# Cross-attention row maxima from the high parts alone, two heads at a time, in a fused decoder layer

## The reference, cut to what matters

```python
k = src_key.reshape(b, s, NUM_HEAD, HEAD_DIM)          # 8, 512, 8, 64
q = tgt_trans.reshape(b, t, NUM_HEAD, HEAD_DIM)
scores = jnp.einsum('bthd,bshd->bhts', q, k) / np.sqrt(HEAD_DIM)
scores = jnp.where(src_mask[:, None, None, :] == 0, -jnp.inf, scores)
attn = jax.nn.softmax(scores, axis=-1)
tgt_update = jnp.einsum('bhts,bshd->bthd', attn, v).reshape(b, t, OUT_SIZE)
```

## Time and profile before

| | |
|---|---|
| median of 3 runs | 2109.98 us (2108.62 to 2110.39) |
| the profiled execution: its own time | 2113.0 us |
| its span, first to last instruction | 2111.2 us |
| mean granted clock of TensorE over the span | 0.975 of full speed |
| PE busy | 1977.4 us (94%) |
| DVE busy | 1397.5 us (66%) |
| ACT busy | 784.5 us (37%) |
| rounds of `phase_b` | first from about 985 us; the loop's seven take 132.8 us each |

### The profile page before, as it was taken

How to read it: one execution, slowest core, us unless ns; L and a number is a source line. 1 busy time by engine, 2 the same in 40 slices (tenths; PEclk the granted TensorE clock), 3 DMA queues, 4 the chain that set the end, 5 groups by cost and what they waited for, 6 DMA issues and landing times. The chain is left out here.

```text
span 2111.2 us, 35399 instructions
## 1 busy us (share of the span) xinstructions
PE 1977.4 (94%) x13100; PEld 1057.0 (50%) x13100; DVE 1397.5 (66%) x1826; ACT 784.5 (37%) x1209; POOL 216.2 (10%) x416
## 2 busy tenths in 40 slices
PE   6999999999999999876789999999999999999998
PEld 5555455545555445533454545545455454554543
DVE  4279978987797879996666555565555555646531
ACT  3322222122222222112655536355363562645622
POOL 0000122003200321031000010100100001000010
PEclk8999999999999999986999999999999999999999
DMA  6112222122122212315641131410414104141010
GB/s 210 36 46 70 76 66 65 61 71 75 55 64 66 81 56 66 111 59 120 194 86 51 27 94 27 96 50 19 96 34 96 50 12 100 36 96 30 1 40 20
DMA packets 151569, 143.10 MB, mean 68 GB/s; under 512 B 55529, under 2 KB 108777, under 8 KB 151426
## 3 DMA queue, kind: packets, MB, share of 16 engines
q1 hardware_dynamic: 147056, 140.58, 23.5%
q10 hardware_dynamic: 4370, 0.34, 0.2%
HBM read 94.75 MB, written 33.55 MB: 61 GB/s over the span
## 5 line engine op out<-in xcount | busy, mean ns | idle before, releaser
L1459 DVE TENSOR_TENSOR p_lo<-k,p_hi 128x1024 f16<-128x1024 f32 x128 | 156.8, 1225 | 194.0 <-ACT p_hi L1347 194.0
L1148 PE MATMUL b_ff<-x2T_hi,w1T_hi 128*128 128x512 f16 x512 | 194.9, 381 | 1.9 <-DVE x2T_lo L1459 1.9
L1504 DVE CUSTOM_DVE_ANT_0 junk<-b_sx,mneg 128x512 f16<-128x512 f32 x256 | 175.7, 686 | 30.4 <-issue 22.3
L1148 PE MATMUL b_ff<-x2T_lo,w1T_hi 128*128 128x512 f16 x512 | 194.9, 381 | 0.0
L1148 PE MATMUL b_ff<-x2T_hi,w1T_lo 128*128 128x512 f16 x512 | 194.7, 380 | 0.0
L1379 ACT ACTIVATE k<-b_st,mbias 128x512 f32<-128x512 f32 x256 | 161.5, 684 | 14.1 <-PE b_st L1192 14.0
L572 PE MATMUL pj_b<-winT_hi,xT_hi 128*128 128x512 f16 x384 | 146.5, 381 | 7.6 <-DVE xT_lo L790 7.6
L1347 ACT ACTIVATE p_hi<-k 128x1024 f16<-128x1024 f32 x128 | 135.3, 1057 | 44.1 <-PE b_av L1207 41.7
L814 DVE TENSOR_TENSOR prod<-q,k 128x4096 f32<-128x4096 f32 x32 | 141.2, 4411 | 8.8 <-ACT bd L696 8.8
L572 PE MATMUL pj_b<-winT_lo,xT_hi 128*128 128x512 f16 x384 | 145.9, 380 | 0.0
L572 PE MATMUL pj_b<-winT_hi,xT_lo 128*128 128x512 f16 x384 | 145.9, 380 | 0.0
(11 more groups left out here) (262 smaller groups left out, 4285.2 us busy)
## 6 DMA issues: line engine op xcount, KB each, us to landing
cn<-in_ctx_dram SPq DMA_DIRECT2D x64, 256.0 KB, 2.8
k<-kT_scratch SPq DMA_DIRECT2D x24, 512.0 KB, 7.8
xn<-in_x_dram SPq DMA_DIRECT2D x32, 256.0 KB, 2.9
xres<-in_x_dram SPq DMA_DIRECT2D x32, 256.0 KB, 2.9
x_scratch<-x SPq DMA_DIRECT2D x32, 256.0 KB, 2.0
q<-x_scratch SPq DMA_DIRECT2D x8, 1024.0 KB, 5.6
q<-x_scratch SPq DMA_DIRECT2D x32, 256.0 KB, 4.2
out_dram<-q SPq DMA_DIRECT2D x32, 256.0 KB, 4.4
```

Of the source, the lines that this page charges most:

```text
L1148: mm = pe.matmul(out, a, c, start=(start and n == 0), stop=end)
L1459: dve.tensor_tensor(dst, bank, hi, ALU.subtract).then_inc(out, 1)
L1504: dve.tensor_tensor_reduce(junk[:, :], sx_b[tt % 2][:, :], mneg[:, :], 1.0, NEG, ALU.add, ALU.max, mx[:, h % 2, tt:tt + 1]).then_inc(s["sx ...
```

## The change

The scores that serve only to find the row maxima are made from the high parts alone: queries high times keys high, with a contraction of 64. Their operands are the natural layouts, `qn` and a new tile `kn` (keys of one batch, high part, 512 KB, loaded by a transfer of its own ahead of the three others). Two heads lie in the two halves of the 128 partitions, so one call of `scores(b, p, tt)` issues two matmuls, one on rows 0 to 63 and one on rows 64 to 127 of the array, for the heads 2p and 2p+1, into two banks at once. The scores that the probabilities are made of are not changed.

`maximum_rows` now serves a pair of heads: `mz` has two columns for the two heads, four matmuls give two rows, and one ACT copy writes both rows for both heads (2 partitions x 1024 elements, in place of 1 x 512). `k2` gets a one in row 64 for even heads and in row 65 for odd ones.

A pair's scores must be complete before its first head goes on. So four calls (eight matmuls, eight DVE passes) now stand ahead of head 0, where one head's four stood: calls 0 and 1 within the last query product, call 2 behind it, and call 3 inside `heads`, after the first feed-forward tile. Calls 1 and 3 go to the banks `b_st`. During the heads, two calls stand in each of the heads 0 to 5 and none in 6 and 7.

```diff
+    kn = sb("kn", [P, 4, B], F16)
...
-    mz = sb("mz", [P, 8, DV], F16)
+    mz = sb("mz", [P, 8, D2 + 2], F16)
...
+    score_banks = lambda p, tt: st_b if p == 0 and tt % 2 else sx_b
...
+                sp.dma_start(kn[:, :, :], kn_in[b, 0]).then_inc(s["k_ld"], 16)
                 sp.dma_start(k1[0:D2, :, :], k_in[b, 0]).then_inc(s["k_ld"], 16)
...
-            def scores(b, h, half):
-
-                for tt in (2 * half, 2 * half + 1):
-                    if h or tt >= 2:
-                        pe.wait_ge(s["sx_max"], 32 * b + 4 * h + tt - 1)
-                    pe.matmul(sx_b[tt % 2][:, :], q1[:, h, tt * P:(tt + 1) * P], k1[:, h, :], start=True,
-                              stop=True).then_inc(s["sx_filled"], 1)
-
-            def maximum_row(b, h):
-                pe.wait_ge(s["negm"], 8 * b + h + 1)
+            def scores(b, p, tt):
+
+                if p:
+                    pe.wait_ge(s["sx_max"], 32 * b + 8 * p + 2 * tt)
+                elif tt >= 2:
+                    pe.wait_ge(s["sx_max"], 32 * b + 2 * tt - 2)
+                for a, bank in enumerate(score_banks(p, tt)):
+                    head = slice(a * D2, (a + 1) * D2)
+                    mm = pe.matmul(bank[:, :], qn[0][head, p, tt * P:(tt + 1) * P], kn[head, p, :], start=True,
+                                   stop=True)
+                mm.then_inc(s["sx_filled"], 1)
+
+            def maximum_rows(b, p):
+                pe.wait_ge(s["negm"], 4 * b + p + 1)
                 for tt in range(4):
-                    mm = pe.matmul(mr_b[0:DV, tt * P:(tt + 1) * P], mz[:, 4 * (h % 2) + tt, :], ident16[:, :],
+                    mm = pe.matmul(mr_b[0:D2 + 2, tt * P:(tt + 1) * P], mz[:, 4 * (p % 2) + tt, :], ident16[:, :],
...
                 feed_forward1(ff, 0)
                 pe.wait_ge(s["q_masked"], 4 * b + 4)
-                maximum_row(b, 0)
+                scores(b, 0, 3)
+                maximum_rows(b, 0)
                 for h in range(H2):
                     for g, (i, _) in enumerate(GROUPS):
                         for a in range(2):
-                            if h + 1 == 2 * i + a:
+                            if h == 2 * i + a:
                                 pe.wait_ge(qs_ld[g][a], 48 * (b + 1))
-                    if h + 1 < H2:
-                        scores(b, h + 1, 0)
+                    following = h // 2 + 1
+                    if following < 4:
+                        scores(b, following, 2 * (h % 2))
                     transposed_scores(b, h, 0)
...
+                    if h % 2 and following < 4:
+                        maximum_rows(b, following)
                     if h + 1 < H2:
-                        maximum_row(b, h + 1)
                         feed_forward1(ff, 2 * h + 2)
...
-                pe.wait_ge(qs_ld[0][0], 48 * (b + 1))
+                pe.wait_ge(s["q_hi"], 4 * b + 2)
                 scores(b, 0, 0)
+                scores(b, 0, 1)
                 queries(b, 3, slice(8, None))
-                scores(b, 0, 1)
+                scores(b, 0, 2)
...
-            def maximum_row(b, h):
-                act.wait_ge(s["mr_filled"], 8 * b + h + 1)
-                act.activation(q2[D2:DV, h, :], mr_b[D2:DV, :], ACT.Copy).then_inc(s["mr_copied"], 1)
+            def maximum_rows(b, p):
+                act.wait_ge(s["mr_filled"], 4 * b + p + 1)
+                act.activation(q2[D2:D2 + 2, 2 * p:2 * p + 2, :],
+                               mr_b[D2:D2 + 2, :].unsqueeze(1).to_broadcast([2, 2, B]),
+                               ACT.Copy).then_inc(s["mr_copied"], 1)
...
             def heads(b, ff):
                 w1_low(ff, 0)
+                maxima(b, 0, 3)
...
-                maximum(b, 0, 0)
+                maxima(b, 0, 0)
                 queries_low(b, 2)
+                maxima(b, 0, 1)
                 queries_masked(b, 3)
-                maximum(b, 0, 1)
+                maxima(b, 0, 2)
                 queries_low(b, 3)
```

More of the change, by code:

```diff
@@ L974, in phase_b @@
     junk = sb("junk", [P, B], F16)
-    mx = sb("mxb", [P, 2, 4], F32)
+    mx = sb("mxb", [P, 4, 2], F32)
     ph = pair("p", [P, 4, B])
@@ L1014, in phase_b @@
     k_in = w.kT_d.rearrange("b z (h d) s -> b z d h s", h=H2)
+    kn_in = w.kT_d.rearrange("b z (o p) s -> b z p o s", p=P)
     v_in = w.v_d.rearrange("b z (st p) o -> b z p st o", p=P)
@@ L1186, in transposed_scores @@
                     if st == 0:
-                        pe.wait_ge(s["mr_copied"], 8 * b + h + 1)
+                        pe.wait_ge(s["mr_copied"], 4 * b + h // 2 + 1)
                     if h or st >= 2:
@@ L1271, in heads @@
                         values(b, h - 1)
-                    if h + 1 < H2:
-                        scores(b, h + 1, 1)
+                    if following < 4:
+                        scores(b, following, 2 * (h % 2) + 1)
                     feed_forward1(ff, 2 * h + 1)
                     transposed_scores(b, h, 1)
+                    if h % 2 and following < 4:
+                        maximum_rows(b, following)
                     if h + 1 < H2:
-                        maximum_row(b, h + 1)
                         feed_forward1(ff, 2 * h + 2)
@@ L1306, in queries_and_first_scores @@
                     pe.wait_ge(s["x2t_lo"], 4 * ff + 2)
[L1307 to L1308 removed]
+                pe.wait_ge(s["k_ld"], 64 * (b + 1))
+                pe.wait_ge(s["q_hi"], 4 * b + 2)
                 scores(b, 0, 0)
+                scores(b, 0, 1)
                 queries(b, 3, slice(8, None))
[L1311 removed]
+                scores(b, 0, 2)
             def x2_transposes(b):
@@ L1326, in _ @@
             queries_and_first_scores(0, None)
-            pe.wait_ge(s["rows_made"], 3)
+            pe.wait_ge(s["rows_made"], 4)
             pe.wait_ge(s["made"], 2)
@@ L1402, in heads @@
                     exponentials(b, h, 1)
-                    if h + 1 < H2:
-                        maximum_row(b, h + 1)
+                    if h % 2 and h + 1 < H2:
+                        maximum_rows(b, h // 2 + 1)
                     exponentials_high(b, h, 1)
@@ L1432, in _ @@
             act.wait_ge(s["cols_ld"], 32)
-            act.wait_ge(s["rows_made"], 3)
+            act.wait_ge(s["rows_made"], 4)
             heads(0, None)
@@ L1495, in queries_low, with maxima @@
                 low(qn[1][:, i, :], qf[i % 2][:, :], qn[0][:, i, :], s["q_hi"], 4 * b + i + 1, s["q_lo"])
[L1497 to L1502, removed]
-                    stand_alone(dve, alone["dve"])
[L1504 to L1508, removed]
+            def maxima(b, p, tt):
+                dve.wait_ge(s["sx_filled"], 16 * b + 4 * p + tt + 1)
+                for a, bank in enumerate(score_banks(p, tt)):
+                    if p or tt or a:
+                        dve.wait_ge(s["sx_max"], 32 * b + 8 * p + 2 * tt + a)
+                    stand_alone(dve, alone["dve"])
+                    dve.tensor_tensor_reduce(junk[:, :], bank[:, :], mneg[:, :], 1.0, NEG, ALU.add, ALU.max,
+                                             mx[:, tt, a:a + 1]).then_inc(s["sx_max"], 1)
+                if tt == 3:
+                    dve.wait_ge(s["sx_max"], 32 * b + 8 * p + 8)
+                    dve.tensor_scalar(mz[:, 4 * (p % 2):4 * (p % 2) + 4, D2:D2 + 2], mx[:, :, :], -1.0, None,
                                       ALU.mult).then_inc(s["negm"], 1)
@@ L1541, in heads @@
                 w1_low(ff, 0)
+                maxima(b, 0, 3)
                 for h in range(H2):
-                    if h + 1 < H2:
-                        maximum(b, h + 1, 0)
+                    following = h // 2 + 1
+                    if following < 4:
+                        maxima(b, following, 2 * (h % 2))
                     if h:
                         normalized(b, h - 1)
-                    if h + 1 < H2:
-                        maximum(b, h + 1, 1)
+                    if following < 4:
+                        maxima(b, following, 2 * (h % 2) + 1)
                     exponentials_low(b, h, 0)
@@ L1599, in _ @@
                     dve.wait_ge(s["rows_made"], 2)
-                    dve.tensor_scalar(k2[D2:P, :, :], q2[D2:P, :, :], w.ident[D2:P, D2:D2 + 1], None,
-                                      ALU.add).then_inc(s["rows_made"], 1)
+                    for a in range(2):
+                        dve.tensor_scalar(k2[D2:P, a::2, :], q2[D2:P, a::2, :], w.ident[D2:P, D2 + a:D2 + a + 1], None,
+                                          ALU.add).then_inc(s["rows_made"], 1)
                 weights_low(lo, om_b[n % 4], high, s["wq_hi"], n + 1, s["wq_lo"])
```

## The result

The changed kernel takes 2149.4 us (median of 4 runs, 2145.7 to 2153.6) against 2110.2 us in 4 runs of the kernel before: a ratio of 1.0189, with a 95% interval of 1.0176 to 1.0202. It is 39 us slower; the forecast was 2141 us, 31 us slower. The profiled execution took 2149.8 us, with a span of 2148.0 and a mean granted clock of 0.969.

What follows compares the result with a forecast made beforehand. PE, busy 94% of the span, plus its waits, bound the kernel; DVE had no slack at the front. Seven rounds at +4.3 us (+30) and batch 0's +1.3 made +31.5: 2141 us, 8-in-10 range 2124 to 2157.

Steps and rivals of the forecast that it cites:

- the rivals: Clock stays up, 2132 us (14%); pairs run one after another, 2154 (14%); front cheap, kernel faster (3%); no change (3%).
- its own terms: Bounds on front (3.0 to 4.2), copy (0.59 to 1.18), clock (0 to 1.7) and batch 0: 2130 to 2150 us.
- The front: Round's start, before head 0's transposed scores: four more DVE passes and a longer copy delay them, +3.66 us a round.
- The heads: Within heads 0 to 6, shorter and longer stretches together: a gain of 0.86 us a round.
- The even stretches: Last transposed scores to values, heads 0, 2, 4: PE's own 4.75 us sets them, -0.39 us each.
- the odd ones: Last transposed scores to values, heads 1, 3, 5: ACT's longer copy makes the chain 5.59 us, +0.45 each.
- Head 6's -0.61: Last transposed scores to values in head 6: the chain sets it and loses its copy, -0.61 us a round.
- The pair absent behind its values: Matmuls behind head 6's values, on PE's path, no longer there: -0.43 us a round.
- The pairs: Two half-depth score matmuls side by side between full ones: no gain, +0.01 us each, +0.1 us a round.
- The clock: Behind the front's wait the clock drops to 1.2 GHz in 8 of 10 rounds: +1.35 us a round.
- The loads ahead of this cost nothing: Key loads ahead of the front: 512 KB more hidden by projections and output_rest; uncovered, up to 7.8 us.
- Batch 0: Same front, but a later wait for a transfer, whose issue moves by 1.3 us, leaves +1.3 us, bounds 0 and +4.

Runs made afterwards that it cites:

- Experiment 2: Changed kernel without DVE's four passes over the second head's scores in each first pair, the negation using the first head's maxima for both: 2117.3 us, 1.0037.
- Experiments 3 and 4: ACT's row copy moved behind p_hi: in the changed kernel (3), 2140.8 us, 1.0148; in the kernel before (4), 2098.7 us, 0.9940.
- Experiment 6: Changed kernel with its order, but each score matmul at full depth of 128 from q1 and k1: 2150.7 us, 1.0190.
- experiment 7: Changed kernel with both matmuls of a call at depth 64 on the same half of the array's rows: 2165.3 us, 1.0257.
- experiment 5: Changed kernel with 13 matmuls of unused result in each batch, between the last pair and the maxima matmuls: 2136.8 us, 1.0121.
- Experiment 1: Kernel before with only the new 512 KB kn transfer for each batch, loaded, waited for and never read: 2117.9 us, 1.0032.
- experiment 8: Changed kernel with kn loaded for batch 0 only, later batches taking maxima from batch 0's keys: 2145.6 us, 1.0169.

## Why the prediction was right, and where it was short

The result lies 8 us above the forecast and inside the range, and none of the rivals came in. It is at the upper end of the 2130 to 2150 that the prediction gave its own terms. With all its bounds at their ends together these come to about 2116 and 2153, so that span was drawn narrower than its sum, without saying how.

- **The front: right.** The wait at `mz` is 3.15 us (3.2 forecast), the copy 1.01 us (1.04), the delay +3.72 (+3.66). Experiment 2 takes the passes away and the delay with them, but for 0.8 us: 0.4 of it is the longer copy, and the rest stays open.
- **The heads: right.** The even stretches end on PE's own 4.75 us, as forecast, the odd ones on the chain through ACT at 5.64 (5.59). Experiments 3 and 4 show that chain by moving the copy off it. Head 6's -0.61 was -0.49. The chain sets it, as forecast, for `values` still waits 0.19 us for p_lo there (the next row), but the chain got shorter by 0.49 only. The pair absent behind its values gave -0.44 (-0.43). What the even heads gain, the odd ones give back, +0.3 us a round more than that.

```profile
1336.38 0.20 PE L1212 MATMUL b_av<-v_hi,p_hi 128*128 128x65 f16 x1 [0.19 <-DVE p_lo L1473]
```

- **The pairs: right.** 0.63 us for two, by the way in and out. Experiment 6 shows that full depth costs the same, and 7 that the gain of working side by side is real and is just eaten up. The rule that a change of tiling mode drains TensorE (the Trainium skill, "TensorEngine Tiling (Array Packing)", Key Properties) has its price here: 0.10 us on each side of a pair.
- **The clock: right mechanism, too small.** I took 1.67 us at 8 rounds in 10, or +1.35. It was every round, and 2.1 us a round by experiment 5; in the round shown the low level held for 6.8 us, as in five of the seven, and for 3.4 in the others. The gap I had read the loss from the earlier trace rows was one of the short kind.
- **The step that failed: "The loads ahead of this cost nothing".** The cover was there, but the transfer lengthens the queue into the start of the next round, and PE's first instruction there comes late. Experiment 1 gives 7 us for it alone, 4.6 of them in the wait at the loop's way back and 2.7 in the second wait, which the changed kernel has not; experiment 8 gives some 4 within the changed kernel, and "last" shows +0.7 a round. I had priced a transfer by who waits for its data, and nobody does; what waited was behind it. The first instruction starts a fixed time behind a packet of instructions, and that packet comes later where the loop has the transfer. That the two go together is shown; what links them is not.
- **Batch 0**: +0.6 measured, +1.3 forecast. The front is 4.8 us longer there, and waits for transfers behind it give most of that back: the longest shrank from 4.0 us to 0.8, since the transfer's issue had moved by 1.6 us only (1.3 in the prediction).

Clock (+5 us in seven rounds), transfer (+5) and head 6 (+1) are the 11 us by which the rounds ran over the forecast; 5.7 us of variation ahead of the first score hid half of them in the profiled execution. All parts together are 42.5 us, where the medians show 39; that the result lies so near the forecast is in part luck.

## What to carry to other kernels

Count what a batching edit must finish before the first consumer can start: here half the array work per score was saved for nothing, while four more vector passes ahead of the first head cost 5 us a round, in the wait and in the clock behind it. Packing a single pair of half-depth matmuls between full ones gains nothing; only from the second pair in a row on is a matmul saved. And look first at what stands between a producer and the wait that ends last: moving one 0.59 us copy behind the step that PE's wait hangs on gave 12 us.

## What the runs showed of the hardware

- Filling a wait of 3.15 us with matmuls whose results nobody reads made the kernel 12.6 us faster; the stretch behind the wait fell from 6.11 to 4.00 us with the granted clock at full.
- Waits of 1.24 and 0.79 us with a pair and four small matmuls between them (experiment 2) left the clock at its full level in all seven rounds; 3.15 and 0.57 to 0.79 us brought it down every time, for 3.4 or 6.8 us.
- A transfer of 512 KB that is never read cost 7 us in eight batches (experiment 1).
- At the loop's way back PE's first instruction started 1.57 to 1.79 us behind the landing of a 16 KB packet of instructions, 60 times in 60.
- Two matmuls on different halves of the array's rows started 3 or 4 ns apart (the changed kernel); two on the same half 0.21 to 0.23 us (experiment 7).
- A copy of 2 partitions x 1024 elements took 1.01 us, against 0.59 for 1 x 512, and 128 x 1024 took 1.06: in these copies the row's length counted, and the partitions hardly.
